# Head sums of a recurrent layer as one task of sixteen small matmul tiles over four PSUM banks

## The reference

```
xn  = layernorm(x);  sx = shift by one token(xn)
x5  = xn + sx * (maa + tanh((xn + sx*maa_x) @ w1) @ w2)      # five mixed inputs
w   = exp(-exp(decay + tanh(x5[1] @ d1) @ d2))               # decay per channel
r, k, v = x5[3] @ Wr.T, x5[0] @ Wk.T, x5[2] @ Wv.T;  g = silu(x5[4] @ Wg.T)
for each token t, each head:
    a   = k_t (outer) v_t
    out = r_t . (u * a + s);   s = a + w_t * s               # u = faaaa, s a 16 x 16 state
x   = x + (groupnorm of out per head * gn_w + gn_b) * g @ Wo.T
xk, xr = mixes of layernorm(x) with its shifted form
x   = x + sigmoid(xr @ fWr.T) * (square(relu(xk @ fWk.T)) @ fWv.T)
```

## Time and profile before

| what | us |
|---|---|
| median of 3 runs | 1547.56 (1545.41 to 1550.09) |
| profiled execution, first to last instruction (its span) | 1549.0 |
| PE busy | 1505.6 (97%) |
| VectorE busy | 898.2 (58%) |
| GpSimd busy | 595.1 (38%) |
| ScalarE busy | 516.3 (33%) |

### The profile page before, as it was taken

How to read it: one execution, slowest core, us unless ns; L and a number is a source line. 1 busy time by engine, 2 the same in 40 slices (tenths; PEclk the granted TensorE clock), 3 DMA queues, 4 the chain that set the end, 5 groups by cost and what they waited for, 6 DMA issues and landing times.

```text
span 1549.0 us, 50439 instructions
## 1 busy us (share of the span) xinstructions
PE 1505.6 (97%) x22156; PEld 1093.0 (71%) x22156; DVE 898.2 (58%) x1990; ACT 516.3 (33%) x910; POOL 595.1 (38%) x528
## 2 busy tenths in 40 slices
PE   8998999999999999999999999999999999999798
PEld 7876866767777676867767677676866767777464
DVE  3658566466665646666465655655666465654542
ACT  1323423333332333423333332333423333342332
POOL 3354425244262533526144261533525244262321
PEclk9999999999999999999999999999999999999999
DMA  7011102011020211102011010201102011020110
GB/s 295 17 44 42 39 8 72 17 39 53 26 61 8 66 26 36 54 6 75 17 39 53 27 54 14 67 26 35 55 5 75 17 39 53 13 62 7 45 42 27
DMA packets 56442, 68.01 MB, mean 44 GB/s; under 512 B 23264, under 2 KB 40032, under 8 KB 55200
## 3 DMA queue, kind: packets, MB, share of 16 engines
q1 hardware_dynamic: 56224, 64.79, 13.6%
HBM read 43.75 MB, written 8.39 MB: 34 GB/s over the span
## 4 chain that ended last, share of the span: by engine, by line
PE 91%; ACT 2%; DVE 2%; issue 2%; SPq 1%; POOL 1%; DMA 0%; ACTq 0%; DVEq 0%; POOLq 0%
PE pair L1195 32%; PE pair L1214 21%; PE at_ps L1124 5%; PE pair L1206 4%; PE at_ps L1117 4%; PE att_ps L1186 3%; PE pair L1222 3%; PE pair L1238 2%; PE pair L1259 2%; PE pair L1300 2%; PE att_ps L1173 2%; PE pair L1302 2%; PE att_ps L1382 1%; DVE x L746 1%; PE pair L1307 1%
## 5 line engine op out<-in xcount | busy, mean ns | idle before, releaser
L1195 PE MATMUL pair<-x,wts 128*128 128x256 f32 x1760 | 402.1, 384 | 0.2 <-POOL x L512 0.2
L1195 PEld LDWEIGHTS pair<-x,wts 128*128 128x128 f32 x1760 | 328.7, 191 | 49.2 <-issue 6.8
L512 POOL TENSOR_TENSOR x<-x,xnT 128x1024 f32<-128x1024 f32 (+1 forms) x79 | 155.8, 1973 | 242.7 <-DVE x L746 242.7
L746 DVE SCALAR_TENSOR_TENSOR x<-pair,vecs,sx 128x256 f32<-128x256 f32 x316 | 130.5, 477 | 189.0 <-PE pair L1238 91.8
L947 ACT ACTIVATE at<-at_ps 128x512 f32<-128x512 f32 x128 | 76.0, 594 | 295.8 <-PE at_ps L1124 258.1
L1195 PE MATMUL pair<-yT,wts 128*128 128x256 f32 x512 | 117.5, 383 | 1.5 <-DVE yT L838 1.5
L1214 PE MATMUL pair<-wts,cen 128*128 128x512 f32 x240 | 114.1, 618 | 2.7 <-DVE x L746 2.5
L1124 PE MATMUL at_ps<-rm,kc 128*16 128x128 f32 (+1 forms) x2048 | 110.5, 275 | 2.9 <-issue 2.9
L1214 PE MATMUL pair<-wts,yT 128*128 128x512 f32 x240 | 111.4, 607 | 0.0
L1214 PE MATMUL pair<-wts,sx 128*128 128x512 f32 x240 | 109.1, 598 | 0.0
L1195 PEld LDWEIGHTS pair<-yT,wts 128*128 128x128 f32 x512 | 94.9, 190 | 16.2 <-DVE gT L782 3.0
(11 more groups left out here) (210 smaller groups left out, 2611.6 us busy)
## 6 DMA issues: line engine op xcount, KB each, us to landing
rm<-rst SPq DMA_DIRECT2D x1024, 12.0 KB, 1.8
xu<-in_x SPq DMA_DIRECT2D x16, 512.0 KB
wts<-in_wts SPq DMA_DIRECT2D x8, 1024.0 KB, 13.7
kvs<-in_s SPq DMA_DIRECT2D x32, 256.0 KB, 3.0
s<-in_s SPq DMA_DIRECT2D x32, 256.0 KB, 3.0
x<-in_x SPq DMA_DIRECT2D x15, 512.0 KB, 4.2
out<-sx SPq DMA_DIRECT2D x15, 512.0 KB, 2.9
prev<-in_prev SPq DMA_DIRECT2D x32, 4.0 KB, 3.9
```

Of the source, the lines that this page charges most:

```text
L512: gp.tensor_tensor(t, t, old, ALU.add).then_inc(x5_ready, 1)
L746: last = ve.scalar_tensor_tensor(seqs(mixed(name, a), g), ps[:, :, g * L:(g + 1) * L], vecs[:, vec, g:g + 1], seqs(sx, g), ALU.add, ALU.mult)
L1195: last = pe.matmul(ps[:, g // 2, TB * (g % 2):TB * (g % 2 + 1)], wts[:, m, k, g * P:(g + 1) * P], source[:, k, :], start=(k == 0), stop=(k ...
```

## The change

The two tasks of a sequence's head sums become one task `hs_b`, and the transposes of v stand alone as `vt_b`. The three inputs lie side by side in one tile `lag` of 320 columns for each group (u·r·k 0 to 127, the other pair 128 to 255, the neighbours 256 to 319). `hs_b` has sixteen matmuls, one for each strip of 32 rows (`quad`, two heads) and each group; each uses a 32x32 tile of the array, with row strip `quad` and column strip `(quad + g) % 4`, and writes 320 columns of PSUM bank `quad`. So the result of one task lies over all four banks, that is over both buffers, and the task waits for the readers of both and holds both until VectorE's third read.

A head thereby leaves PE on another partition strip than the one in which it came. The value side is laid out to match: the columns of Wv and Wg, the rows of Wo and the group norm's vectors are put in another order (`of_v`), the read-out and the state products write and read by `v_quad` and `v_pair`. The part "all" of the chain of b=1, until now at the end of the former step in two pieces (`bonv1`, `pairs1`) with a buffer of its own, moves into the step that uses it; `hs_0` too is a task of the step of its block. All engines but SyncE have new orders.

```diff
+LAG2, LAG1, LAGW = L, 2 * L, 2 * L + L // 2
...
-    "wv": -2, "c02_1": 0, "c1v_1": 0, "yT": -1, "wo": -1, "x2T": -1, "kk": -1, "rr": -1,
+    "wv": -2, "hs_0": 0, "hs_1": 0, "vt_1": 0, "yT": -1, "wo": -1, "x2T": -1, "kk": -1, "rr": -1,
     "xT": 2, "h": 2,
-    "bonv1": 1, "pairs1": 1, "chain1": 1, "chain1b": 0, "chain1c": 0, "chain0": 1, "chain0b": 1, "chain0c": 1, "rch1": 0, "rch1b": 0, "rch0": 1, "rch0b": 1,
+    "chain1": 0, "chain1b": 0, "chain1c": 0, "chain0": 1, "chain0b": 1, "chain0c": 1, "rch1": 0, "rch1b": 0, "rch0": 1, "rch0b": 1,
...
-PE_ORDER = ["kt0", "V7", "mixWV", "kv0", "A0", "wv.0", "aT1", "V0", "wv.1", "A1", "c02_1", "V1", "c1v_1", "A2", "v.0",
...
+PE_ORDER = ["V7", "kt0", "hs_0", "A0", "kv0", "mixWV", "aT1", "V0", "wv.0", "wv.1", "A1", "vt_1", "V1", "hs_1", "A2", "V2",
...
-POOL_ORDER = ["mixV", "mixW", "rch1", "gn_sub", "c02_1", "wv", "bon1", "rch1b", "mixK", "gn_scale", "mixR", "ln1_stats",
...
+POOL_ORDER = ["hs_0", "bon0", "mixV", "gn_sub", "hs_1", "mixW", "rch1", "wv", "rch1b", "bon1", "mixK", "gn_scale",
...
-        pair = [ctx.enter_context(nc.psum_tensor(f"pair{p}", [P, 2, 512], F32)) for p in range(2)]
+        pairs = ctx.enter_context(nc.psum_tensor("pairs", [P, 4, 512], F32))
+        pair = [pairs[:, 2 * p:2 * p + 2, :] for p in range(2)]
...
-            freed[f"c02_{b}"] = [(m2_ready, 2, b + 1)]
-            freed[f"c1v_{b}"] = [(m1_ready, 2, b + 1), (vtm_ready, 2, b + 1)]
+            freed[f"hs_{b}"] = [(m1_ready, 2, b + 1)]
+            freed[f"vt_{b}"] = [(vtm_ready, 2, b + 1)]
+
+        def v_quad(g, quad):
+
+            return (quad + g) % 4
+
+        def v_pair(g, quad):
+
+            return 4 * quad + v_quad(g, quad)
...
-                    for g in range(G):
-                        last = ve.scalar_tensor_tensor(bonv(blk, b)[:, g, :], rb[:, g, :], vecs[:, FAAAA, g:g + 1],
+                    for g in range(G):
+                        last = ve.scalar_tensor_tensor(lag[:, g, 0:L], rb[:, g, :], vecs[:, FAAAA, g:g + 1],
                                                        kb[:, g, :], ALU.mult, ALU.mult)
...
-                    ve.tensor_tensor(bonv(a, b)[:, :, :].rearrange("p g t -> p (g t)"), ps[:, 0, :],
-                                     vT[:, b, :, :].rearrange("p g t -> p (g t)"), ALU.mult)\
-                      .then_inc(m0_ready, 1)
-                    v4 = vT[:, b, :, :].rearrange("p g (f q) -> p (g f) q", q=4)
-                    ve.tensor_tensor(p2[:, :].rearrange("p (f i j) -> p f i j", i=2, j=2),
-                                     ps[:, 1, :].rearrange("p (f i j) -> p f i j", i=2, j=2),
-                                     v4[:, :, 0:2].unsqueeze(2).broadcast_to([P, G * 32, 2, 2]), ALU.mult)\
+                    if a.past(2, b - 1):
+                        ve.wait_ge(aT_done, a.count(2, b - 1))
+                    ve.tensor_tensor(bonv[b][:, :, :], pairs[:, :, 0:L], vT[:, b, :, :], ALU.mult).then_inc(m0_ready, 1)
+                    v4 = vT[:, b, :, :].rearrange("p g (f q) -> p g f q", q=4)
+                    ve.tensor_tensor(lag[:, :, LAG2:LAG1].rearrange("p g (f i j) -> p g f i j", i=2, j=2),
+                                     pairs[:, :, LAG2:LAG1].rearrange("p g (f i j) -> p g f i j", i=2, j=2),
+                                     v4[:, :, :, 0:2].unsqueeze(3).broadcast_to([P, G, 32, 2, 2]), ALU.mult)\
                       .then_inc(m2_ready, 1)
-                elif name in ("c1v_0", "c1v_1"):
-                    b = int(name[-1])
-                    ve.wait_ge(done[name], a.count(1, 1))
-                    ve.tensor_tensor(p1[:, :], ps[:, 0, 0:G * L // 2],
-                                     vT[:, b, :, :].rearrange("p g (f q) -> p (g f) q", q=2)[:, :, 0],
+                    ve.tensor_tensor(lag[:, :, LAG1:LAGW], pairs[:, :, LAG1:LAGW],
+                                     vT[:, b, :, :].rearrange("p g (f q) -> p g f q", q=2)[:, :, :, 0],
                                      ALU.mult).then_inc(m1_ready, 1)
...
-                    pe.matmul(o[32 * quad:32 * quad + 32, 0, :], s0[:, g, 32 * quad:32 * quad + 32],
+                    to = 32 * v_quad(g, quad)
+                    pe.matmul(o[to:to + 32, 0, quad, :], s0[:, g, 32 * quad:32 * quad + 32],
                               rst[:, b, g, R64A:RST], start=(g == 0), stop=False, skip_group_check=True)
...
-                elif name in ("c02_0", "c02_1"):
+                elif name in ("hs_0", "hs_1"):
                     b = int(name[-1])
                     pe.wait_ge(kchain, a.count(2 * NK, NK * b + 6))
-                    pe.matmul(ps[:, 0, :], headall[:, :], bonv(a, b)[:, :, :].rearrange("p g t -> p (g t)"),
-                              start=True, stop=True)
-                    last = pe.matmul(ps[:, 1, :], headall[:, :], p2[:, :], start=True, stop=True)
-                elif name in ("c1v_0", "c1v_1"):
+                    for quad in range(4):
+                        rows_ = slice(32 * quad, 32 * quad + 32)
+                        for g in range(G):
+                            to = 32 * v_quad(g, quad)
+                            last = pe.matmul(pairs[to:to + 32, quad, 0:LAGW], headall[rows_, rows_], lag[rows_, g, :],
+                                             start=True, stop=True)
+                elif name in ("vt_0", "vt_1"):
                     b = int(name[-1])
-                    pe.wait_ge(kchain, a.count(2 * NK, NK * b + 2))
                     pe.wait_ge(v_ready, a.count(1, 1))
-                    pe.matmul(ps[:, 0, 0:G * L // 2], headall[:, :], p1[:, :], start=True, stop=True)
-                    for g in range(G):
-                        last = pe.transpose(ps[:, 1, g * P:(g + 1) * P], vT[:, b, g, :], ident[:, :])
+                    for g in range(G):
+                        last = pe.transpose(ps[:, 0, g * P:(g + 1) * P], vT[:, b, g, :], ident[:, :])
...
+    slot, quad, sub = [a.ravel() for a in np.meshgrid(range(4), range(4), range(32), indexing="ij")]
+    of_v = P * ((quad - slot) % 4) + 32 * slot + sub
+    mats = [w["Wr"].T, w["Wk"].T, w["Wv"].T[:, of_v], w["Wg"].T[:, of_v], w["Wo"].T[of_v, :],
```

More of the change, by code:

```diff
@@ L60 @@
-BANK_SECOND = {0: BANK | {"c02_1": 1, "c1v_1": 0}, 1: BANK | {"c02_1": 1}}
+BANK = {"mixW": 0,
+ "mixV": 1,
+ "wv": 1,
+ "vt_1": 0,
+ "v": 0,
+ "mixK": 1,
+ "mixR": 0,
+ "z": 1,
+ "k": 1,
+ "yT": 0,
+ "decay": 0,
+ "mixG": 1,
+ "r": 0,
+ "xT": 1,
+ "wo": 1,
+ "g": 0,
+ "x2T": 1,
+ "vt_0": 1,
+ "kk": 0,
+ "rr": 1,
+ "h": 1}
+TASKS = list(BANK) + ["hs_0", "hs_1"]
+BANK_FIRST = {"mixK": 1,
+ "mixW": 0,
+ "mixR": 1,
+ "k": 0,
+ "z": 1,
+ "decay": 1,
+ "r": 0,
+ "mixV": 1,
+ "mixG": 1,
+ "v": 0,
+ "g": 1,
+ "xT": 0,
+ "h": 0,
+ "vt_0": 1}
@@ new lines @@
+ACT_ORDER = ["kt0", "dec0", "E0", "att1", "E1", "vtm1", "gn_square", "E2", "gn_std", "v", "E3", "kt1", "z", "dec1", "yT",
+ "k", "decay", "E4", "xT", "r", "E5", "E6", "x2T", "g", "h", "att0", "E7", "vtm0", "kk", "rr"]
+DVE_ORDER = ["attb1", "hs_0", "kv0", "mixV", "mixW", "gn_sum", "chain1", "wv", "ln1_stats", "hs_1", "gn_var", "chain1b",
+ "gn_rec", "chain1c", "mixK", "kv1", "mixR", "attb0", "mixG", "ln1", "chain0", "xT", "wo", "ln2_stats", "ln2",
+ "x2T", "g", "chain0b", "xr", "chain0c"]
+POOL_ORDER = ["hs_0", "bon0", "mixV", "gn_sub", "hs_1", "mixW", "rch1", "wv", "rch1b", "bon1", "mixK", "gn_scale",
+ "ln1_stats", "mixR", "yT", "mixG", "rch0", "ln2_stats", "rch0b"]
@@ new lines @@
+PE_EDGE = {-1: ["mixKW", "mixR", "k.0", "z", "k.1", "decay", "r.0", "mixV", "r.1", "mixG", "v.0", "v.1", "g.0", "xT", "g.1",
+      "h", "vt_0"],
+    LAST: ["kt0", "V7", "kv0", "hs_0", "aT1", "A0", "wv.0", "vt_1", "V0", "wv.1", "A1", "V1", "hs_1", "A2", "kt1", "V2",
+      "A3", "kv1", "yT", "V3", "A4", "aT0", "wo.0", "V4", "A5", "yT@0", "wo.1", "A6", "V5", "wo@0", "x2T", "V6",
+      "A7", "x2T@0", "V7+", "kk.0", "aT1+", "kk.1", "kk@0", "rr.0", "yT@1", "rr.1", "rr@0"],
+    LAST + 1: ["wo@1", "wv.0", "x2T@1", "wv.1", "kk@1", "wv@0", "rr@1", "wv@1"]}
@@ new lines, in build, with readers_before @@
+        turn_of = {turn_: n for n, turn_ in enumerate(turns)}
+        def bank(name, step):
+            return pair[0 if (name, step, 0) in turn_of else 1]
+        def readers_before(name, step, at_):
+            out = []
+            for which in (0, 1):
+                n = turn_of.get((name, step, which))
+                if n is None:
+                    continue
+                for name_, step_, other in reversed(turns[:n]):
+                    if other == which:
+                        blk = at_.plus(AHEAD[name_] + step_ - step)
+                        if name_ in MIXES:
+                            out.append((mix_ready, blk.count(5, turn_no(name_, blk) + 1)))
+                        else:
+                            out += [(semaphore, blk.count(per, more)) for semaphore, per, more in freed[name_]]
+                        break
+            return out
```

177 lines of the change are left out of this document (69 added, 108 removed).

## The result

| | kernel before | changed kernel |
|---|---|---|
| median of the runs, us | 1546.94 (1545.41 to 1550.09, 4 runs) | 1586.28 (1579.66 to 1589.21, 4 runs) |
| profiled execution, span, us | 1549.0 | 1587.3 |
| mean granted clock of PE | 0.995 | 0.973 |

The changed kernel takes 1.0231 times as long, with a 95% interval of 1.0206 to 1.0256: 39 us slower. The direction was forecast and 1563 was not: 1586 lies 4 us above the range.

What follows compares the result with a forecast made beforehand. TensorE (PE), busy 97% of the span, was taken as the bound. Step 88.8+0.5+3.6+1.1 = 94.0 us against 92.58, times 13 = +18.5, −3 for start and end: 1564.5, or 1563 on the runs' scale; range 1513 to 1582.

Steps and rivals of the forecast that it cites:

- PE's work: PE in a full step without waits: 92.02−4.68+1.5 = 88.8 us, with 0.75 us for each head-sum task.
- The decisive wait: Behind hs_1, GpSimd's back-to-back work delays VectorE's chain to 14.8 us; PE waits 3.6 us over kt1 and z.
- The clock: After the new pauses PE runs at half clock, costing 1.5 us in three of four steps: +1.1 a step.
- The step as a whole: One full step from start to next start: 94.0 us forecast, against 92.58 in the kernel before.
- start and end: Steps outside the 13 full ones, four with head sums: −3 us taken, between −13 and +6.
- the edits at nothing: New channel order and moved chain1 cost nothing; chain1 finds VectorE partly idle some 10 us ahead of hs_1.
- the chain is late, the clock stays: Rival: VectorE's chain delays PE without clock loss; step 92.9 us, time 1549 (1540 to 1556), chance 0.19.
- the chain is not late: Rival: VectorE's chain ends in time behind hs_1; step 90.3 us, time 1515 (1505 to 1535), chance 0.31.

## Why the prediction was wrong

- *PE's work*: right. 88.8 us a step was laid, 88.77 measured; 0.75 for the task, 0.82 and 0.75 measured.
- *The decisive wait*: right in mechanism, place and size of its cause (chain end 14.8, measured 14.67). At kt1 and z PE then waits 1.40+0.91 = 2.3 us (2.6 in the mean of the twelve steps), not 3.6, in part because it arrives later: about 1 us had gone in the pauses ahead of V2, whose new place had been costed at nothing, and xT waits 0.58 us more. All pauses of an undisturbed step are 93.56−88.77 = 4.8 us, 4.1 was laid.
- *The clock*: right in kind, a little small. Laid 1.1 us a step or 13 in twelve; measured 15.6 more than before, in ten stretches, which lie in nine of the twelve steps: three of four, as laid.
- *The step as a whole*, the first of two terms of the sum that were too small: 94.0 laid, 95.44 measured as mean of twelve. Of the 1.4 us between, 1.0 is pauses (61.7/12 = 5.1 for 4.1) and 0.4 the clock (18.3/12 = 1.5 for 1.1). The pause at kt1 changes from step to step, from 1.05 to 2.16 us, which a walk through one step does not show.
- *The step that failed: start and end.* I took −3 us; with +1.4 for the thirteenth full step that is −1.6, and +11.0 was measured. The sentence behind it is in the edits at nothing: chain1 was to find room on VectorE in the step that it moved into. That holds in a full step, where hs_1 never waits for chain1. In step 0 it did not: hs_1 waits 4.29 us for it. In the last step VectorE's list has gn_var, wv and hs_1 ahead of the chain's other two parts, and PE waits 7.48 us at kt1. Outside the twelve steps there are 47 us at half clock where there were 13. The upper end of +6 kept for this was priced from the waits of a full step. The runs put 6.7 of the 12.6 us on the last step; how the others divide no run shows.

Together: +10.3 from the twelve steps (27.3 for 12×1.42 = 17.0) and +12.6 from the rest make the 23 us between 1563 and 1586; counted from z to z, the two are +14.5 and +8.3. Either alone would have left the time in the range, which ended at 1582.

- *The rivals*: "the chain is late, the clock stays" is what the run with filled pauses comes near to, at 1574, not 1549; "the chain is not late" has its own run, the one with the early mix addition, and took 1548, not 1515. What that rival had too small is the rest of the waits, 1.5 us a step laid and 3.0 to 3.1 measured without the clock's disturbance, and again start and end: outside its twelve steps that run has +6.7 us against the kernel before.

By the Trainium skill ("TensorE: Matmul & The Clock Gate", Part 1) an idle engine falls back to the lower clock. The trace agrees only in part: after 1.97 and 0.91 us of pauses the clock fell (the stretch at 838.97), after 1.40 and 0.91 in the step shown it did not.

```profile
836.58 0.66 PE L1164 MATMUL kv_ps<-ident,k 128*128 128x128 f32 x4 [1.97 <-DVE k L731]
838.14 1.23 PE L1305 MATMUL pairs<-x,dec 128*64 128x128 f32 x16 [0.91 <-DVE x L778]
```

Why a given pause lowers the clock and another does not stays open.

## What to carry to other kernels

When work is moved in an engine's list, look at what it will stand in a row with, and which engine that row locks out: two names moved on GpSimd, which is idle 60% of a step, cost some 36 us here, nearly all that the change takes from PE. A moved task has to be costed in the first and the last steps too, where the engines that hide it have other loads. And before filling one pause, look at what the moved piece waits for itself.
